# Second attention of a two-layer block: the mask is added on TensorE and the softmax reads PSUM; another order of transpositions in the first

## The reference, cut to what matters

```python
q = _split_heads(query @ Wq.T + bq)
k = _split_heads(key @ Wk.T + bk)
v = _split_heads(value @ Wv.T + bv)
scores = jnp.einsum('bhqd,bhkd->bhqk', q, k) / math.sqrt(D_K)
scores = jnp.where(mask[:, None, :, :] == 0, -1000000000.0, scores)
p_attn = jax.nn.softmax(scores, axis=-1)
x = jnp.einsum('bhqk,bhkd->bhqd', p_attn, v)
```

## Time and profile before

| | us |
|---|---|
| median of 3 runs (lowest, highest) | 761.55 (760.32, 763.07) |
| the profiled execution, its own time | 761.38 |
| its span, first to last instruction | 759.5 |
| PE busy | 713.4 (94%) |
| DVE busy | 447.8 (59%) |
| ACT busy | 368.2 (48%) |
| POOL busy | 277.0 (36%) |

### The profile page before, as it was taken

How to read it: one execution, slowest core, us unless ns; L and a number is a source line. 1 busy time by engine, 2 the same in 40 slices (tenths; PEclk the granted TensorE clock), 3 DMA queues, 4 the chain that set the end, 5 groups by cost and what they waited for, 6 DMA issues and landing times.

```text
span 759.5 us, 15888 instructions
## 1 busy us (share of the span) xinstructions
PE 713.4 (94%) x4674; PEld 586.3 (77%) x4675; DVE 447.8 (59%) x1662; ACT 368.2 (48%) x1240; POOL 277.0 (36%) x335
## 2 busy tenths in 40 slices
PE   8999999899998999999999899998988999999994
PEld 5788888656666888888866588777865999999993
DVE  4799999449946433433445799999973222223321
ACT  2899999422222555554552788887831121221220
POOL 1022111000033555555507677771103343434421
PEclk9899999999999999999999999999998999999998
DMA  7543334320034555555963247774511656455540
GB/s 178 199 146 110 128 105 153 120 68 22 7 104 79 162 162 161 164 160 159 132 124 94 67 129 208 222 213 139 155 56 47 217 182 202 152 202 188 173 132 6
DMA packets 64328, 103.08 MB, mean 136 GB/s; under 512 B 20161, under 2 KB 42129, under 8 KB 64004
## 3 DMA queue, kind: packets, MB, share of 16 engines
q1 hardware_dynamic: 52996, 74.19, 31.2%
q0 software_dynamic: 10976, 27.22, 14.3%
q10 hardware_dynamic: 288, 0.79, 0.3%
HBM read 82.83 MB, written 22.07 MB: 138 GB/s over the span
## 4 chain that ended last, share of the span: by engine, by line
PE 69%; DVE 19%; issue 5%; ACT 4%; DMA 1%; POOL 0%; DVEq 0%; another core or an unknown queue 0%; ACTq 0%; SPq 0%; POOLq 0%
PE bank L1502 11%; PE bank L1517 10%; PE bank L1448 8%; PE bank L991 7%; PE bank L1461 4%; PE bank L897 3%; PE bank L966 3%; PE bank L1331 2%; PE bank L975 2%; PE bank L937 2%; PE bank L1439 2%; DVE X L1625 2%; DVE U L1816 2%; DVE R L2051 2%; DVE mx L1634 1%
## 5 line engine op out<-in xcount | busy, mean ns | idle before, releaser
L720 ACT ACTIVATE U<-U,mx 128x77 f32<-128x77 f32 x512 | 134.6, 350 | 17.0 <-issue 8.2
L651 POOL DMA_INDIRECT U<-normed,idx_all x95 | 90.4, 952 | 140.4 <-PE bank L1439 71.4
L1448 PE MATMUL bank<-R,U 128*128 x380 | 98.2, 381 | 0.0
L1502 PE MATMUL bank<-X,R 128*128 128x128 f32 x736 | 85.9, 275 | 0.0
L1502 PEld LDWEIGHTS bank<-X,R 128*128 128x128 f32 x736 | 84.1, 192 | 0.1
L1517 PE MATMUL bank<-R,X 128*128 (+1 forms) x368 | 83.1, 379 | 0.0
L2185 DVE TENSOR_TENSOR U<-U,bank 128x128 f32<-128x128 f32 x95 | 27.3, 287 | 84.3 <-issue 77.3
L1517 PEld LDWEIGHTS bank<-R,X 128*128 128x128 f32 x368 | 68.2, 190 | 8.4
L604 POOL DMA_INDIRECT R<-expert_out,slot x64 | 62.2, 972 | 33.0 <-DMA expert_out<-xr 16.9
L1448 PEld LDWEIGHTS bank<-R,U 128*128 128x128 f32 x380 | 64.8, 190 | 5.3
L2213 DVE TENSOR_SCALAR X<-bank,U 128x128 f32<-128x128 f32 x92 | 25.9, 344 | 64.6 <-PE bank L1502 47.3
(11 more groups left out here) (262 smaller groups left out, 1510.6 us busy)
## 6 DMA issues: line engine op xcount, KB each, us to landing
R<-in_w SPq DMA_DIRECT2D x21, 1024.0 KB
R<-in_w SPq DMA_DIRECT2D x40, 256.0 KB
R<-in_gu SPq DMA_DIRECT2D x8, 1024.0 KB, 5.4
expert_out<-U SPq DMA_DIRECT2D x48, 128.0 KB
expert_out<-xr SPq DMA_DIRECT2D x47, 128.0 KB
normed<-xr SPq DMA_DIRECT2D x32, 128.0 KB
R<-in_down SPq DMA_DIRECT2D x8, 512.0 KB, 3.7
x<-X SPq DMA_DIRECT2D x16, 128.0 KB
```

The lines of the kernel that those rows point to most:

```text
L651: pool.indirect_dma_start(xg0[i % NXG], None, xn_d[0], bass.IndirectOffsetOnAxis(idx_all[:, i:i + 1], 0)).then_inc(EX[0]["gath"][i % NXG], 16)
L720: ins = act.activation(sc[u][:, h * S2:(h + 1) * S2], sc[u][:, h * S2:(h + 1) * S2], ACT.Exp, bias=mx[u][:, h:h + 1])
L1448: mm = pe.matmul(bank[2 + u][:, 0:2 * F0], xgT0[u][:, c, :], gu_w[:, c, bass.ds(e, 1), :].rearrange("p a n -> p (a n)"), start=(c == 0), s ...
L1502: mm = pe.matmul(bank[1 + 2 * v + f // 4][:, (f % 4) * P:(f % 4 + 1) * P], w1_of[v][:, c, f * P:(f + 1) * P], xgT1[v][:, c, :], start=(c = ...
```

## The change

In the second attention:

- PE first writes the mask into each of banks 0 to 3, as a product of a bf16 identity (`ident16`) with a bf16 mask (`mask16`) of the tile, repeated for four heads: four matmuls of 128 x 308 in bf16. The mask is 0 or a large negative number, as before.
- On top of it PE accumulates the scores, now in quarter-arrays as in the first attention: eight matmuls of 128 x 154 with 32 rows of contraction (`head_scores`, for both layers). The weights' columns and biases are permuted on the host for it, and the block-diagonal keys have half the size.
- DVE no longer copies scores (but for tile 0). It takes the maxima from the banks, four heads at a time: four reductions of 128 x 308. ACT's exponentials read the banks and write `sc` (but for tile 0).
- The banks are free only when the exponentials have read them: `scores1` waits on `TL["exp"]`, which ACT raises after each half of the exponentials.
- ACT's order in a step: the first half of the exponentials of tile t + 1 comes ahead of everything, then `xT`, then the copies of `pT`; PE does `transpose_p` 0 and 1 one after the other, ahead of `rows_turned`, and `queries` ahead of `last_blocks`.

In the first attention `transpose_p(1)` is moved ahead of `rows_turned`, on ACT both copies of `pT` come ahead of `xT`, the scores wait for both halves of `copied` at once, and `keep_busy` is spread anew: in step 14 two and then three that were not there, in step 15 two ahead of `weigh` and seven in place of nine behind the scores.

```diff
                     for h in range(8 * g, 8 * g + 8):
-                        ins = act.activation(sc[u][:, h * S2:(h + 1) * S2], sc[u][:, h * S2:(h + 1) * S2],
-                                             ACT.Exp, bias=mx[u][:, h:h + 1])
+                        p_of = sc[u][:, h * S2:(h + 1) * S2]
+                        s_of = bank[h // HG][:, h % HG * S2:(h % HG + 1) * S2] if l == 1 and t >= 0 else p_of
+                        ins = act.activation(p_of, s_of, ACT.Exp, bias=mx[u][:, h:h + 1])
+                    if l == 1:
+                        ins.then_inc(TL["exp"], 1)
...
+                def head_scores(t, first):
+                    for c in range(KC):
+                        for g in range(NG):
+                            r = slice(QR * g, QR * g + QR)
+                            mm = pe.matmul(bank[g][:, c * QH * S2:(c + 1) * QH * S2], qT[r, c, :],
+                                           kbd[l][r, batch(t, 2) * KC + c].rearrange("p h k -> p (h k)"),
+                                           start=first, stop=True, skip_group_check=True)
+                            if c == KC - 1 and g % 2:
+                                mm.then_inc(T["sc_mm"], 1)
...
+                def scores1(t, n):
+                    k = t + 2
                     for g in range(NG):
+                        if k > 1 and g % 2 == 0:
+                            pe.wait_ge(TL["exp"], 2 * k - 1 + g // 2)
+                        pe.matmul(bank[g][:, 0:HG * S2], ident16[:, :],
+                                  mask16[:, k:k + 1, :].to_broadcast([P, HG, S2]),
+                                  start=True, stop=False, skip_group_check=True)
+                    pe.wait_ge(T["q"], n + 3)
+                    head_scores(t, False)
...
                 def step0(t):
                     if on(t, 0):
                         pe.wait_ge(T["p"], n + 1)
                         transpose_p(n, u, 0)
+                        transpose_p(n, u, 1)
                     if on(t, 2):
                         rows_turned(n, par(2))
-                    if on(t, 0):
-                        transpose_p(n, u, 1)
...
+                    if t in (NT - 2, NT - 1):
+                        pe.wait_ge(T["copied"], 2 * NT)
+                        keep_busy(2, 0)
                     if on(t, 0):
                         weigh(t, n)
+                    if t == NT - 2:
+                        keep_busy(3, 0)
...
                     if t == NT - 1:
-                        pe.wait_ge(T["copied"], 2 * NT)
-                        keep_busy(9, 0)
+                        keep_busy(7, 0)
...
                 def step1(t):
+                    if on(t, 2):
+                        queries(n)
                     if on(t, 0):
                         last_blocks(n, u)
-                    if on(t, 2):
-                        queries(n)
...
-                    if on(t, 1) and t != -1:
-                        maxima(n + 1, par(1), 1)
...
                         for g in range(2):
                             dve.wait_ge(T["sc_mm"], 2 * n + 5 + g)
-                            for a in range(2):
-                                q = 2 * g + a
-                                ins = dve.tensor_tensor(s3[:, HG * q:HG * q + HG, :],
+                            for q in (2 * g, 2 * g + 1):
+                                ins = dve.tensor_reduce(mx[par(2)][:, HG * q:HG * q + HG],
                                                         bank[q][:, 0:HG * S2].rearrange("p (h k) -> p h k", h=HG),
-                                                        bt.to_broadcast([P, HG, S2]), ALU.add)
+                                                        AX.X, ALU.max, negate=True)
+                            ins.then_inc(T["mx"], 1)
```

More of the change, by code:

```diff
@@ L222, in build @@
         iota16 = sb("iota16", [P, P], BF16)
+        ident16 = sb("ident16", [P, P], BF16)
         part_id = sb("part_id", [P, 1])
@@ L927, in attention @@
             def attention(l):
-                T, W = AT, attn_w[l]
+                T, TL, W = AT, ATL[l], attn_w[l]
+                if l == 1:
+                    pe.wait_ge(KV["mask"], 1)
                 if l == 0:
@@ L1021, in output_turned @@
                     mm.then_inc(T["ot_mm"], 1)
-                def scores0(t, n):
-                    pe.wait_ge(T["q"], n + 3)
-                    for c in range(KC):
-                        for g in range(NG):
-                            if c == 0 and g % 2 == 0:
-                                need(pe, T["copied"], 2 * n + 3 + g // 2)
-                            r = slice(QR * g, QR * g + QR)
-                            mm = pe.matmul(bank[g][:, c * QH * S2:(c + 1) * QH * S2], qT[r, c, :],
-                                           kbd[0][r, batch(t, 2) * KC + c].rearrange("p h k -> p (h k)"),
-                                           start=True, stop=True)
-                            if c == KC - 1 and g % 2:
-                                mm.then_inc(T["sc_mm"], 1)
                 def step0(t):
@@ L1130, in step1 @@
                     if on(t, 2):
-                        scores(t, n)
+                        scores1(t, n)
                     if t == -1:
@@ L1220, in last_tile1 @@
                 pe.wait_ge(T["ot"], n)
-                pe.wait_ge(T["copied"], 2 * n + 3)
+                pe.wait_ge(T["copied"], 2 * NT + 3)
                 for c in range(4):
@@ L1660, in step0 @@
                         dve.tensor_copy(iota16[:, :], iota[:, :])
+                        dve.tensor_copy(ident16[:, :], ident[:, :])
                     if t == FIRST - 3:
@@ L2265 @@
             m = a[f"L{l}_xattn_{w}"]
-            arrays[f"L{l}_{w}"] = rows_of((m[quarters] if l == 0 and w in ("Wq", "Wk") else m).T)
+            arrays[f"L{l}_{w}"] = rows_of((m[quarters] if w in ("Wq", "Wk") else m).T)
     arrays["bias0"] = rows_of(a["fside_1x1xSxS2_0"].reshape(S, S2))
     arrays["mask1"] = rows_of(a["mask_BxSxS2_if1"].reshape(N, S2))
-    arrays["bqk"] = np.stack([a["L1_xattn_bq"].reshape(KC, P).T, a["L1_xattn_bk"].reshape(KC, P).T], 1)
+    arrays["bqk"] = np.stack([a[f"L1_xattn_{b}"][quarters].reshape(KC, P).T for b in ("bq", "bk")], 1)
     arrays["bv"] = a["L1_xattn_bv"].reshape(1, D)
```

89 lines of the change are left out of this document (41 added, 48 removed).

## The result

| | us |
|---|---|
| changed kernel, median of 4 runs (lowest, highest) | 768.13 (767.75, 769.13) |
| before, median of 4 runs | 762.31 (760.32, 763.44) |
| ratio, 95% interval | 1.0074 [1.0040, 1.0108] |
| profiled execution of the changed kernel, its own time / its span | 767.75 / 765.9 |

The change made the kernel 5.8 us slower; 5.3 us faster was forecast, and 768 lies outside the range. That holds for the occasion of these runs. In three later sessions the same kernel is about 1% faster than before, while the kernel before took the same time in all (medians of 762.2 to 762.9 us). The experiments tell of it, and of how far the reason is known.

A forecast was written before the change was run, and what follows sets the result against it. DVE was taken to bound both attentions, the second passing to a loop through PE, DVE and ACT. Second attention -3.6 us and first -1.7 gave -5.3 on the profiled 761.4, a median of 756.2; range 751.5 to 762.

The forecast's parts named there:

- second rival: Second attention, steps 2 to 6: `weigh` still reported late, +2.5 us, and the clock drops anyway, 760.2 us; chance 0.18.
- scores to first reduction: Second attention's loop: from the start of PE's scores to DVE's first reduction, 0.96 us.
- reductions to exponentials: Second attention's loop: two reductions on DVE, 0.85 us, and 0.03 to ACT's exponentials, 0.88 us together.
- `last_blocks` to ACT's copy: Second attention's loop: from PE's `last_blocks` to ACT's copy, 0.47 us, taken from two transpositions of the output.
- The loop: Second attention: scores, maxima, exponentials, queries, mask and back to scores sum to 8.33 us a step, the new bound.
- Exponentials out of PSUM: Second attention, ACT: 0.21 us each and 0.31 for the last, 1.78 for eight; 2.02 out of SBUF.
- the slower rival: Second attention: exponentials gain nothing from PSUM, the loop is 8.97 us, the time 764.7 to 766.5 us; chance 0.12.
- The gain per step: Second attention: each step falls from 8.72 to 8.33 us, 0.39 less, -5.1 us over 13 steps.
- The start: Second attention, step 0: exponentials of tile 1 come ahead of `xT` on the path to the scores, +1.4 us.
- The order of the first attention: First attention: moved transpositions fill PE's stall, but DVE keeps the steps at 7.54 us, so 0 us.
- The clock: End of the first attention, 135 to 140 us: the new `keep_busy` holds the clock, more likely than not, -1.5 us.
- The tail: Second attention: shorter path behind the last scores, -0.5 us; late reductions in steps with extra DVE work, +0.6 us.

The follow-up runs named there:

- changed_third: The changed kernel as it is, run for the third time, in session 4: 754.41 us, ratio to before 0.9900.
- session 1: Each attention's changes alone (757.71, 769.41 us); changed kernel and kernel before with zeros written instead of gathers (757.90, 766.23 us).
- sessions 1 and 2: Two batches of four kernels, each batch on one chip with its own runs of before: 757.71 to 769.41 us, then 755.11 to 773.01 us.
- before_again: The kernel before as it is, run once more beside the changed kernel: 757.97 us (1 run).
- changed_fourth: The changed kernel as it is, run for the fourth time: 753.73 us (1 run).
- first_half_again: The first attention's changes alone, the second attention as in the kernel before, run again: 758.37 us, ratio to before 0.9954.
- changed_again: The changed kernel as it is, run once more: 753.82 us, ratio to before 0.9878.

## Why the prediction was wrong, by its steps

**The step that failed.** It is this one, of the second rival: "*the late report of `weigh` stays*", with its price of +2.5 us and the words "I found no cause in the trace, so nothing speaks against it but that the distances change". I took the delay for a property of `weigh`. On that occasion it could meet any of PE's reports while gathers were being issued: in step 3 of the first trace those of the scores, the turned output, the rows for routing, the queries and `last_blocks` came 0.7 to 1.1 us behind. In the kernel before, with DVE as the limit, only `weigh`'s had left DVE idle. The change closed a loop that meets PE's reports three times a step, and every link of my sum was priced from a place where reports are prompt: the earlier trace rows lie at 12 to 15 us, where no gather runs, and in the earlier trace rows the report of the turned output, 0.29 us behind, is prompt although a gather begins at 494.71 us. So the terms 0.96 (scores to first reduction), 0.88 (reductions to exponentials) and 0.47 (`last_blocks` to ACT's copy) were 1.26, 1.31 and 1.01 us in step 3 of the first trace, and the loop 9.80 in place of 8.33. Over steps 0 to 12 the first trace has 118.0 against 109.8 us of `changed_third`, and in step -2 12.5 against 9.55. These 11.1 us are more than the whole loss of 5.8, and nearly the 11.9 by which the forecast missed.

What is shown: on the two occasions with late reports (the first runs and session 1) all four traces of kernels with gathers have them, 14 to 27, and the two without these gathers none in the stretch. On the occasions without, the changed kernel is faster. That gathers are needed rests on two kernels of one session, in which the writes put in their place cost time of their own. Whether it takes the loads of weights beside the gathers is open. What isn't shown at all: why the same program on another occasion has none. The chip's number doesn't tell it (sessions 1 and 2 have the same). The traces of the first runs and of session 1 also hold fewer records of landed DMAs (4,724 in the first trace of the changed kernel, 8,112 in `changed_third`). That goes with the occasion and not with the late reports: the two traces without gathers have as few (4,711 and 4,668). So something about the occasion differed even where no report was late; what, no run tells.

**The loop** was right where reports are prompt: 8.33 summed, 8.42 measured in step 3 without late reports, and 8.40 to 8.53 in the steps without gathers even in the first trace. Its terms are in the table; single ones were off by up to 0.12 us in both directions and partly cancel. Exponentials out of PSUM took 1.81 to 1.84 us for eight (1.78 forecast, 2.10 out of SBUF), so the slower rival, that PSUM brings nothing, is wrong. The time came out slower than that rival's 764.7 to 766.5 for another reason. The four reductions took 1.63 us, 0.39 from start to start, as assumed from the additions.

**The gain per step** was too large even so. Without late reports the kernel before has 112.8 us for steps 0 to 12 and the changed one 109.8: -3.0 and not -5.1. Some 1.5 us of the error are the loop, 0.1 in each step. The other 0.5 is that my 8.72 us of before held late reports too: in steps 3 to 5 `before_again` has 8.59, 8.58 and 8.60, the first trace 8.71, 8.68 and 8.70.

**The start**, +1.4: it is 20.02 against 18.45 us for steps -2 and -1 (`changed_fourth`, `before_again`), +1.6, where the clock holds. Where it falls it is +4.3. That PE would have a gap of 2.6 us in step -1, after which the clock can fall, I had not looked at.

**The order of the first attention**, 0: this was wrong in the other direction. Between the scores of step -2 and of step 13 lie 110.1 us in `before_again` and 108.8 in `first_half_again`. The steps near 7.54 did stay, as forecast for all: DVE sets them. But the first four full steps fell from 7.08, 7.52, 7.53, 7.53 to 6.72, 7.13, 7.10, 7.37 and the last from 7.54 to 7.25. I had read the waits of 50 to 120 us alone. **The clock**, -1.5: held from 130 to 140 us, as forecast.

**The tail**, -0.5 + 0.6: from the scores of step 13 to the end +0.8 was measured in the first pair and -2.8 between `before_again` and `changed_fourth`. Most of that stretch is the expert stage, so these small terms can't be judged.

The forecast of 756.2 was 2 us above what the changed kernel takes where reports are prompt (753.8 and 754.4), and 12 below what it took where they were not. That the first is so near is partly luck: the gain per step was overrated by 2 us, the first attention underrated by 1.3, and the clock gave more than was counted on.

## What to carry to other kernels

Before a change closes a loop through several engines, look at how long each engine's updates take to arrive in the stretch where the loop will run, and price every link there, not where the rows are tidy. A stall with no cause in the trace is a reason to look at what other queues do at that time, above all GpSimd's gathers: a kernel with slack at each hand-over hides late reports (the one before took 762.3 us in the first runs and 762.2 to 762.9 later), one without pays each of them. And a comparison on one chip in one session can have the wrong sign for another: repeat the pair elsewhere before keeping or rejecting a change of 1%.

## What the runs showed of the hardware

TensorE's semaphore updates, 0.29 us behind the start of the matmul that carries them as a rule, came 0.7 to 3.6 us behind in traces in which GpSimd issued indirect gathers (0.94 to 1.2 us each, some 1.3 us apart), while those of VectorE and ScalarE kept to 0.01 us. In step 3 of the first trace the held updates came 0.74, 1.5 to 1.6 and 1.73 to 1.77 us after the start of the last gather, in the first trace of the kernel before the five of `weigh` 1.81 to 1.86 us. It happened in the first runs and in session 1, and not in the five sessions after, in which the same gathers were issued.

After an idle time of 2.6 us of TensorE the granted clock was 0.50 for 6.8 us in two traces of the changed kernel (`changed_again`, `changed_third`; it fell 0.5 us after the gap had ended), and 1.00 in another with the same gap (`changed_fourth`). Eight bf16 matmuls of 512 columns in the gap (the trace has seven of them) left 0.91 us of it idle and the clock at 1.00.

Exponentials of 77 columns in a row, with a bias for each row, follow each other by 0.208 us out of PSUM and by 0.250 out of SBUF (medians in the second attention of `changed_third` and of the first trace of before). Reductions of 308 columns out of PSUM follow each other by 0.39 us.

The normalisation `xr` of 128 x 256 on VectorE (L1559 in `changed_third`, SBUF to SBUF) took 0.87 to 0.93 us in three steps in which GpSimd added two tiles of 128 x 256 (L633) beside 0.72 us of it, and 0.40 to 0.46 in steps 1 to 8, in which a gather ran beside it.
